# A two-layer graph attention kernel: edge masks on ScalarE and block transposes on VectorE in place of TensorE transposes

## The reference, cut to what matters

```python
h = jnp.maximum(_layernorm(x, axis=-1), 0.0)
x = x + _L0_gnn_ref(h, L0_gnn_W, L0_gnn_a, adj, 8192)   # layer 0, attention with a threshold, then elu
h = jnp.maximum(_layernorm(x, axis=-1), 0.0)
x = x + _L1_gnn_ref(h, adj, L1_gnn_W, L1_gnn_a)         # layer 1
...
e = jax.nn.leaky_relu(e_src[:, None] + e_dst[None, :], negative_slope=ALPHA)
attention = jax.nn.softmax(jnp.where(adj > 0, e, NEG_INF), axis=1)
h_prime = attention @ Wh
```

## Time and profile before

| | before |
|---|---|
| median of 3 runs | 2136.89 us |
| profiled execution, its time | 2139.07 us |
| profiled execution, its span | 2137.3 us |
| TensorE busy, share of the span | 94% |
| VectorE, ScalarE, GpSimd busy | 73%, 38%, 30% |
| moved by DMA | 447.75 MB |

### The profile page before, as it was taken

One profiled execution on the slowest core, in us unless ns is written; L12 is line 12 of the kernel. 1 busy time (PEld: TensorE's weight loads), 2 busy tenths in 40 slices (PEclk: granted clock), 3 DMA queues, 4 the chain that ended last, 5 costly groups with the idle time before them and its releaser, 6 DMA issues. The chain is left out here.

```text
span 2137.3 us, 43514 instructions
## 1 busy us (share of the span) xinstructions
PE 2010.9 (94%) x17812; PEld 2003.4 (94%) x17812; DVE 1561.5 (73%) x2452; ACT 806.9 (38%) x950; POOL 638.6 (30%) x263
## 2 busy tenths in 40 slices
PE   5699999999999999999965699999999999999997
PEld 4699999999999999999965699999999999999997
DVE  6687777777777777777747677777777777777775
ACT  4677777777777777777734000000000000000000
POOL 0675655575655575656510000000000000000000
PEclk9899999999999999999987799999999999999998
DMA  7889888899888899888832522323222323222230
GB/s 227 331 341 375 318 329 318 334 373 362 334 316 327 323 384 359 323 328 327 331 130 79 190 69 70 99 80 100 80 81 60 98 79 99 80 73 79 68 99 11
DMA packets 112206, 447.75 MB, mean 209 GB/s; under 512 B 8320, under 2 KB 57984, under 8 KB 62592
## 3 DMA queue, kind: packets, MB, share of 16 engines
q1 hardware_dynamic: 112000, 444.89, 56.4%
HBM read 365.04 MB, written 79.82 MB: 208 GB/s over the span
## 5 line engine op out<-in xcount | busy, mean ns | idle before, releaser
L984 PE MATMUL psum<-h_all,arena 128*128 128x129 f32 x8192 | 960.0, 275 | 0.2 <-DVE arena L1007 0.2
L1163 PE MATMUL psum<-h_all,arena 128*128 128x129 f32 x8192 | 919.4, 275 | 24.7 <-DVE arena L1180 24.7
L1163 PEld LDWEIGHTS psum<-h_all,arena 128*128 128x128 f32 x8192 | 917.9, 192 | 26.4 <-issue 17.3
L984 PEld LDWEIGHTS psum<-h_all,arena 128*128 128x128 f32 x8192 | 937.5, 192 | 1.2 <-issue 0.5
L1007 DVE SCALAR_TENSOR_TENSOR arena<-arena,rho_col,psum 128x512 f32<-128x512 uint8 (+1 forms) x1024 | 693.8, 742 | 235.6 <-PE psum L970 218.3
L1180 DVE SCALAR_TENSOR_TENSOR arena<-arena,rho_col 128x1024 f32<-128x1024 f32 (+1 forms) x512 | 653.3, 1284 | 235.4 <-PE psum L1163 222.9
L911 POOL TENSOR_SCALAR arena<-arena 128x2048 uint8<-128x2048 int32 x256 | 637.6, 2526 | 441.8 <-DMA arena<-in_adj_dram 293.4
L929 ACT ACTIVATE arena<-arena 128x2048 bf16<-128x2048 uint8 x256 | 487.8, 1906 | 35.1 <-POOL arena L911 35.1
L940 ACT ACTIVATE arena<-psum 128x1024 uint16<-128x1024 uint16 x256 | 261.1, 1020 | 251.0 <-DVE arena L1007 250.4
L970 PE MATMUL psum<-ident,arena 128*128 128x128 f32 x1024 | 154.4, 274 | 14.5 <-POOL arena L911 14.5
L970 PEld LDWEIGHTS psum<-ident,arena 128*128 128x128 f32 x1024 | 121.1, 142 | 14.7 <-POOL arena L911 14.7
(11 more groups left out here) (100 smaller groups left out, 191.8 us busy)
## 6 DMA issues: line engine op xcount, KB each, us to landing
arena<-in_adj_dram SPq DMA_DIRECT2D x256, 1024.0 KB, 9.8
edgesT<-arena SPq DMA_DIRECT2D x64, 1024.0 KB, 7.6
arena<-edgesT SPq DMA_DIRECT2D x64, 1024.0 KB, 8.8
arena<-r_mid SPq DMA_DIRECT2D x2, 3072.0 KB, 13.8
h_mid<-h_all SPq DMA_DIRECT2D x16, 256.0 KB, 2.3
arena<-in_x_dram SPq DMA_DIRECT2D x16, 256.0 KB, 3.1
arena<-h_mid SPq DMA_DIRECT2D x16, 256.0 KB, 3.9
x_mid<-arena SPq DMA_DIRECT2D x16, 256.0 KB, 2.4
```

Source lines behind the costliest of these rows:

```text
L984: last = nc.tensor.matmul(acc_tile(g, G0, k), wTs[m % WRING][:, k * P:(k + 1) * P], h_all[:, j, :], start=(j == 0 and k % 2 == 0), stop=(j ...
L1163: last = nc.tensor.matmul(acc_tile(g, G1, k), wTs[m % RING][:, k * P:(k + 1) * P], h_all[:, j, :], start=(j == 0 and k % 2 == 0), stop=(j ...
```

## The change: what it does

Both layers now work on 8 groups of 8 row tiles (`G = 8`), with 128 x 1024 weight tiles and a ring of six.

Layer 0 no longer uses GpSimd or TensorE for the edges. A piece of adj is 32 rows of each of four column quarters, 1024 columns wide: `(b i)` on the partitions, 512 KB. ScalarE makes its byte mask with a steep sigmoid and counts the edges in the same instruction; VectorE turns 32 x 32 blocks of words (`nc.vector.transpose`), 8 column tiles at a time, into one of four buffers, from which the weight tiles are formed and the edges stored. A chunk is now 32 column tiles of a group and has 32 pieces; there are 16 chunks. The 32 pieces of the first chunk are masked and turned inside `prepare`, whose ScalarE stream takes them between its own steps. The rows of x, h and the sums are taken in the order in which this puts them, so x is loaded, and the result stored, in four DMAs of 32 partitions.

```diff
+G = 8
+HALVES = 2
+COLS = 2
+LC = N // BK // COLS
+CT = T // COLS
+SBT = 8
+PIECES = HALVES * BK * BK
+NA = 6
+ER = 4
+RING = 6
...
+        adj_in = [part(4 * N - (NA - i) * LC, LC).bitcast(I32) for i in range(NA)]
+        adj_pieces = adj.rearrange("(a t i) (b c n) -> t a c b i n", a=BK, i=BP, b=BK, c=COLS)
...
+        def load_piece(sp, n):
+            g, c, h, k, a = piece(n)
+            if n >= NA:
+                sp.wait_ge(masked, n - NA + 1)
+            sp.dma_start(adj_in[n % NA], adj_pieces[g * G + 2 * k + h, a, c])\
+                .then_inc(adj_in_loaded[n % NA], 16)
+
+        def mask_piece(act, n):
+            g, c, h, k, a = piece(n)
+            act.wait_ge(adj_in_loaded[n % NA], 16 * (n // NA + 1))
+            if n >= PIECES and k == 0 and a == 0:
+                act.wait_ge(turned, turn_number(n // PIECES - 1, h, SUBS - 1))
+            nc.scalar.activation(pack_bytes[h][:, k, a], adj_in[n % NA].rearrange("p (m j) -> p m j", j=BP),
+                                 ACT.Sigmoid, bias=half_step[:, 0:1], scale=STEEP,
+                                 accum_out=cnt[g % 2][:, a, 2 * k + h, c:c + 1]).then_inc(masked, 1)
+
+        def turn_edges(dve, chunk, h, s):
+            block = chunk * SUBS + s
+            if s == 0:
+                dve.wait_ge(masked, chunk * PIECES + (h + 1) * BK * BK)
+            if block >= ER and h == 0:
+                dve.wait_ge(edges_stored[block % ER], 16 * (block // ER))
+            nc.vector.transpose(edge_words[:, block % ER, h],
+                                packs[h][:, s * SBT * P:(s + 1) * SBT * P].rearrange("p (b i) -> p b i", b=SBT))\
+                .then_inc(turned, 1)
...
@@ prepare, scalar @@
+                    if first:
+                        for m in range(NA):
+                            mask_piece(act, m)
                     deviation(0)
                     for q in range(Q):
...
+                        if first:
+                            for m in range(NA + 2 * q, min(NA + 2 * q + 2, PIECES)):
+                                mask_piece(act, m)
...
@@ fast_path_0, sync @@
+                for chunk in range(1, NG * COLS + 1):
+                    for i in range(PIECES):
+                        ahead = chunk * PIECES + i + NA
+                        if ahead < NG * COLS * PIECES:
+                            load_piece(sp, ahead)
+                        if i in (4, 7, 10, 13):
+                            store_block((chunk - 1) * SUBS + (i - 4) // 3)
...
@@ fast_path_0, scalar @@
+                for chunk in range(1, NG * COLS):
+                    for i in range(PIECES):
+                        mask_piece(act, chunk * PIECES + i)
+                        if chunk % COLS == 1 and chunk > 1 and i == 26:
+                            elu(chunk // COLS - 1)
...
@@ fast_path_0, vector @@
+                finish_at = {5: 0, 7: 1, 9: 2, 14: 3, 16: 4}
+                turn_at = {15: (0, 0), 17: (0, 1), 23: (0, 2), 24: (1, 0), 26: (1, 1), 28: (1, 2)}
+                turn_late = {1: (0, 3), 3: (1, 3)}
...
@@ fast_path_1, sync @@
+                load_block(0)
                 load_r(sp, r_loaded, 0)
-                groups_of(sp, NG1, group)
...
```

More of the change, by code:

```diff
@@ L147, in kernel_program @@
         d_mid = nc.dram_tensor("d_mid", [1, N], F32, kind="Internal").ap()
[L149 to L155, removed]
+        edgesT = nc.dram_tensor("edgesT", [NG * NSUB, P, SBT * GW], U8, kind="Internal").ap()
@@ L282, in variance @@
                     def variance(i):
-                        wait(dve, x_loaded[i], 16, 16)
+                        wait(dve, x_loaded[i], 16 * BK, 16 * BK if first else 16)
                         c = slice(i * TQ, (i + 1) * TQ)
@@ L802, in fold, with form_tile, sum_tile, tiles @@
                                     ALU.mult).then_inc(h_folded, 1)
+        def form_tile(g, j, wT):
+            return nc.vector.scalar_tensor_tensor(wT.rearrange("p (k n) -> p k n", k=BK), r_of(g),
+                                                  rho_col[:, j:j + 1], edge_bytes[:, (g * NSUB + j // SBT) % ER, j % SBT],
+                                                  ALU.max, ALU.mult)
+        def sum_tile(g, j, wT):
+            for k in range(G):
+                last = nc.tensor.matmul(acc_tile(g, k), wT[:, k * P:(k + 1) * P], h_all[:, j, :],
+                                        start=(j == 0 and k % 2 == 0), stop=(j == T - 1), skip_group_check=True)
+            return last
+        def tiles(ap):
+            return ap.rearrange("p (t f) -> p t f", t=G)
         def fast_path_0(x_in, x_to):
@@ L845, in fast_path_0 @@
[L845 to L853, removed]
-            def columns_of(ap, it, g):
-                return ap[:, bass.ds(it * G1 + g // 2 * G1, G1)].rearrange("p (k h) -> p k h", h=2)[:, :, g % 2]
@@ new lines, in load_block, with store_out @@
+                def load_block(block):
+                    if block >= ER:
+                        sp.wait_ge(formed, (block - ER + 1) * SBT)
+                    sp.dma_start(edge_blocks[:, block % ER], edgesT[block]).then_inc(edges_loaded[block % ER], 16)
+                def store_out(g):
+                    sp.wait_ge(acc_read, g + 1)
+                    for b, rows in each_quarter():
+                        sp.dma_start(out_view[b, :, g * G:(g + 1) * G, :], tiles(xo)[rows]).then_inc(stored, 16)
@@ new lines, in load_residual @@
+                def load_residual(g):
+                    if g >= 1:
+                        sp.wait_ge(acc_read, g)
+                    sp.dma_start(tiles(xr), x_view[g]).then_inc(res_loaded, 16)
+                load_block(0)
+                load_r(sp, r_loaded, 0)
+                for block in range(1, NG * NSUB):
+                    load_block(block)
+                    if block == 2:
+                        load_r(sp, r_loaded, 1)
+                        load_r(sp, r_loaded, 2)
+                    if block % NSUB == 7:
+                        g = block // NSUB
+                        if g >= 1:
+                            store_out(g - 1)
+                        load_residual(g)
@@ L1212, in finish @@
                     last.then_inc(acc_read, 1)
-                def group(it, g):
+                fold(h_folded, 0)
+                dve.wait_ge(r_loaded[0], 16)
+                for g in range(NG):
                     if g == 1:
```

584 lines of the change are left out of this document (261 added, 323 removed).

## The result

The changed kernel takes 3923.25 us (median of 3 runs, 3921.22 to 3926.84) against 2136.89: 1.836 times as long, 95% interval 1.832 to 1.840. The forecast was 3910. The span of its profiled execution is 3921.4 us, 1784.1 more than before. Layer 0 with its preparation ended at 2910.1 us instead of 1109.9 (+1800.2); from there to the end it is 1011.3 us instead of 1027.4 (-16.1).

What follows compares the result with a forecast made beforehand. TensorE bound both layers before, DMA close behind in layer 0; after the change, adj loads on four DMA engines bind layer 0. Layer 0 2897 + rest 1012 + 1.8 = 3911 us, stated as 3910; range 2190 to 4100.

Steps and rivals of the forecast that it cites:

- Four engines: Adj loads in layer 0, starting with count 4, run on four DMA engines at 25.9 GB/s each: 2799 us; chance 0.62.
- The signs named: Layer 0: DMA share about 0.3 near 125 GB/s, loads landing in about 25 us, masks waiting for adj, TensorE busy a third.
- The chunk: Layer 0: the loads of one chunk last 173 us on four engines.
- Last load to the end of layer 0: Layer 0: 3.7 us before the first transfer, 2799 of loads, 8 for preparation, then the remaining work; end at 2897 us.
- The tail: After layer 0's last load: mask, transpose and tile 3.7 us, 39 weight tiles 70, low clock 3, finishing eight row tiles 10.
- Costs no row had shown: Layer 0: block transpose on VectorE 1.2 us (bounds 0.6 to 2.6), mask with count on ScalarE 1.2 us (1.0 to 1.9).
- Layer 1: From layer 0's end to the kernel's end: still bound by TensorE, 1012 us instead of 1027.4.
- the start: Layer 1: first turned block ahead of `r_row` and 1 MB instead of two, so VectorE starts 8 us earlier.
- the group changes: Layer 1: TensorE idles 7.6 us at seven group changes; two more weight tiles and eight copies fewer save 7 us.
- The first rival: Layer 0 loads use all sixteen engines or a changing four, and the masks' windows bind: 2285 us; chance 0.23.
- both named waits: Layer 0: VectorE's transposes wait for ScalarE at tile 24, and tile 14 for the elu: 12 and 23 us each.
- The second rival: Layer 0 loads use sixteen engines and the masks' windows do not bind: 2090 us, 2045 with no wait; chance 0.12.

Runs made afterwards that it cites:

- the walks of 8 and 4: Kernel before, adj loads' source walked over rows as (8, 16) or (4, 32) instead of 128: 2726.45 us with 8, 8046.0 us with 4 (general path also ran).
- before_ring8: Kernel before with eight weight tiles instead of four in fast_path_1 alone: 2126.95 us, ratio 0.9958.
- rows_first: Changed kernel, each adj piece walked (32 rows, 4 quarters): 7693.26 us with the general path also run; fast path of layer 0 ended at 1431.5 us.
- before_halves: Kernel before with each 1 MB load of adj as two loads of 128 rows x 4 KB: 2136.06 us, ratio 1.0003.
- quarters: Changed kernel with each adj piece loaded by four transfers of 32 partitions, one for a column quarter: 2638.73 us, ratio 1.235.
- 16 x 8 rows: Kernel before with the adj loads' source walked over rows as (16, 8) instead of 128: 2407.66 us, ratio 1.126.

## Why the prediction was right, step by step

**Four engines.** Right, and shown by the walks of 8 and 4 and by the packets under way. It was the choice on which all hung: no row of before bore on it, and it got a chance of 0.62. The rate of one was 26.3 GB/s between two pieces, against 25.9 taken from the earlier trace rows. The signs named came too: a share of 0.33 at 128 GB/s (about 0.3 and 125 said), and TensorE busy 35% of the stretch in layer 0 (a third said). The landing time of the loads can't be read.

**The chunk.** 173 us forecast, 176.0 measured in one chunk, from the first mask of one chunk to that of the next:

```profile
1456.14 1.45 ACT L202 ACTIVATE arena<-arena,half_step 128x1024 uint8<-128x1024 int32 x1 [15.58 <-DVE arena L216]
```
```profile
1632.16 1.45 ACT L202 ACTIVATE arena<-arena,half_step 128x1024 uint8<-128x1024 int32 x1 [15.58 <-DVE arena L216]
```

The pause of about 16 us between chunks is there as well (15.58), and covered: behind it ScalarE takes four pieces that have landed, one every 1.38 us.

**Last load to the end of layer 0.** The last piece was due at 3.7 + 2799 + 8 = 2811 us; its mask began 15 us later, 0.5% of the stage; which of the terms it belongs to was not separated. The tail of 86.7 us was 83.8 (2826.29 to 2910.10):

```profile
2826.29 1.44 ACT L202 ACTIVATE arena<-arena,half_step 128x1024 uint8<-128x1024 int32 x1 [3.50 <-DMA arena<-in_adj_dram]
```
```profile
2901.22 0.17 DVE L1025 TENSOR_SCALAR inv<-psum 128x8 f32<-128x8 f32 x1 [9.23 <-PE psum L899]
...
2910.10 0.41 SPq L942 DMA_DIRECT2D x_mid<-arena  x1
```

**Costs no row had shown.** A block transpose takes 1.24 us (1.2 taken). A mask takes 1.43 us and, with its count beside the next, 1.38 a piece; I had 1.2, too low by 15%, within the bounds. It was worth nothing here, since ScalarE waited for nearly every piece.

**Layer 1.** 1012 us forecast, 1011.3 measured. Of the 16.1 us, 7.1 are the start (first product's wait 17.06 us in the earlier trace rows, 9.98 now), 7.6 the group changes, now gone altogether, and 1.7 less busy time (917.7 against 919.4), together 16.4. The start (VectorE's first tile and TensorE's wait):

```profile
2987.98 1.28 DVE L892 SCALAR_TENSOR_TENSOR arena<-arena,rho_col 128x1024 f32<-128x1024 f32 x1 [5.44 <-DMA arena<-r_mid]
...
2989.41 5.78 PE L899 MATMUL psum<-h_all,arena 128*128 128x129 f32 x26 [9.98 <-DVE arena L892]
```

The row says more than I had: VectorE now waits for `r_row`, not for the edges. The deeper ring by itself gave 8.7 us in `before_ring8`; that the start gains by the order of the loads was read from this trace and not run by itself.

**The first rival.** Its mechanism holds, its size did not. With all sixteen engines in use both named waits appear, and the edits that bring the elu and the masks forward gave 85 and 78 us. But it priced the loads at the 415 GB/s of the earlier trace rows. The kernel nearest to it is `rows_first`, one transfer to 128 partitions for a piece: about 2445 us by the estimate above against its 2285, or the 2325 expected with the measured mask and transpose. Its 4 KB packets took 187 ns in the mean where `before_halves` had 166, and why is open. In `quarters`, at 265 GB/s, the windows of 17.8 to 19.4 MB take 67 to 73 us instead of 43 to 47, and those of 15.2 MB 57 instead of 37: seven times 25 and eight times 20 are 335 us, and 2285 + 335 = 2620 us, where 2638.73 was measured. This sum was made afterwards and leaves the mask at 1.2 us. The second rival (2090) needed 470 GB/s, and no row here shows more than 426; the best kernel on this path, with two queues, stands 12% above before. Not tried: alternating the quarters so that neighbouring transfers go to the two halves of the partitions.

What stays open: why 16 x 8 rows to all 128 partitions, with every engine busy, also gives 270 GB/s. The packets of 8 KB (a fifth of them the stores of turned edges) give a hint. In the kernel before 93% of them take 300 to 320 ns; with the walk of 16 x 8 24% do and the median is 513, and with 32 rows x 8 KB 24% do and the median is 512. Lengths so alike speak for one cause behind both, which then isn't that a transfer reaches only 32 partitions; no run separates the order of the partitions from that of the addresses, and none shows the cause.

## What to carry to other kernels

Read a DMA by its shape before its bytes: the count that its walk starts with can confine it to as many engines, so a load that starts with 4 ran on a quarter of them, and splitting it by partitions mended only part of that: transfers to 32 partitions were slow on all sixteen. In the profile the first shows as a low DMA share while an engine waits for nearly every load, the second as a share of 1.0 at a low rate. And when one half of a change loses 1800 us, look whether the other half gains: the deeper ring alone made the kernel before 0.4% faster.

## What the runs showed of the hardware

- The same 1 MB loads use a share of 0.99, 0.57 or 0.31 of the DMA engines for a first count of 16, 8 or 4.
- A full share doesn't mean a full rate: 337 GB/s at 0.85 for 128 plain rows, 263 to 272 GB/s at 0.99 to 1.00 for transfers to 32 partitions of 4 KB or 8 KB rows and for 16 x 8 rows. The packets are longer: 8 KB in 475 to 478 ns in the mean instead of 322, 4 KB in 253 to 262 instead of 162 to 166.
- With loads on four engines SP's issue of a load takes about as long as the load: 4.8 us in the median in the changed kernel, where the loads come every 4.99 us, against 0.42 with quarters.
- Two queues (SP and GpSimd) moved 281 GB/s with transfers to 32 partitions, where one moved 263.
